# Causal attention: the masked score rows of two heads issued side by side, and whole and masked rows alternating in the order of the maxima

## The reference

```
q, k, v = einsum('bte,hed->bhtd', x, Wq), the same with Wk, Wv     # B 8, T 1024, H 16, d 16
scores = einsum('bhtd,bhsd->bhts', q, k)
scores = where(tril(ones(T, T)), scores, -inf) / sqrt(E)           # E 256
w = softmax(scores, axis=-1)
out = einsum('bhts,bhsd->bhtd', w, v)
```

## Time and profile before

| | |
|---|---|
| median of 3 runs | 5279.27 us (5270.48 to 5296.33) |
| profiled execution | 5293.36 us |
| its span in the trace | 5291.6 us |
| mean granted TensorE clock | 0.892 |
| causal attention in that span | to 1571 us, the steps from 135.6 us |

### The profile page before, as it was taken

How to read it: one execution, slowest core, us unless ns; L and a number is a source line. 1 busy time by engine, 2 the same in 40 slices (tenths; PEclk the granted TensorE clock), 3 DMA queues, 4 the chain that set the end, 5 groups by cost and what they waited for, 6 DMA issues and landing times. The chain is left out here.

```text
span 5291.6 us, 68269 instructions
## 1 busy us (share of the span) xinstructions
PE 4637.5 (88%) x23444; PEld 2457.6 (46%) x23444; DVE 3439.4 (65%) x6212; ACT 2705.4 (51%) x3205; POOL 1377.1 (26%) x1043
## 2 busy tenths in 40 slices
PE   5999999999976888888888888888878999999999
PEld 3544444444433544455445544555543444444443
DVE  5566566656647888878887888455545565565653
ACT  1444444445453344443444344122227888888888
POOL 1011111111112332233233332000004545455454
PEclk7787778778787998999899899999989999999999
DMA  6233222322310000000000000000016766666664
GB/s 166 60 74 64 73 62 62 86 62 72 72 37 15 0 0 0 0 0 0 0 0 0 0 0 0 13 1 0 0 31 156 162 153 144 162 146 154 152 146 110
DMA packets 145900, 322.06 MB, mean 61 GB/s; under 512 B 39504, under 2 KB 64480, under 8 KB 129264
## 3 DMA queue, kind: packets, MB, share of 16 engines
q1 hardware_dynamic: 137664, 310.88, 25.6%
q10 hardware_dynamic: 7920, 7.87, 0.5%
q0 software_dynamic: 64, 0.05, 0.0%
HBM read 237.93 MB, written 80.74 MB: 60 GB/s over the span
## 5 line engine op out<-in xcount | busy, mean ns | idle before, releaser
L1714 ACT ACTIVATE gelu_out<-hidden,b_col 128x1024 f32<-128x1024 f32 x1024 | 1085.4, 1111 | 171.1 <-PE hidden L1628 169.9
L529 ACT ACTIVATE probsT<-scoresT 128x1024 f32<-128x1024 f32 (+3 forms) x768 | 603.8, 810 | 609.7 <-PE scoresT L467 603.9
L577 DVE TENSOR_REDUCE maxima<-front 128x1 f32<-128x512 f32 (+3 forms) x1280 | 735.7, 630 | 274.4 <-PE front L439 177.7
L1694 POOL TENSOR_TENSOR combined<-combined,gated 128x512 f32<-128x512 f32 x480 | 615.6, 1283 | 679.0 <-DVE gated L1812 679.0
L918 POOL TENSOR_TENSOR pair_sums<-sims 128x1024 f32<-128x1024 f32 x256 | 487.9, 1913 | 1140.0 <-DVE pair_exp L1032 777.3
L1812 DVE SCALAR_TENSOR_TENSOR gated<-expert_out,b_col,gates_spread 128x512 f32<-128x512 f32 x480 | 359.1, 748 | 452.1 <-PE expert_out L1638 246.7
L1628 PE MATMUL hidden<-slice_stack,w_stack 128*128 128x512 f32 x2048 | 626.9, 428 | 14.1 <-ACT gelu_out L1714 14.1
L433 PE MATMUL front<-k_stack,q_stack 48*128 48x512 f32 (+3 forms) x1536 | 541.3, 493 | 62.2 <-DVE maxima L577 35.6
L1638 PE MATMUL expert_out<-gelu_out,w_sb 128*32 128x512 f32 x4096 | 547.2, 606 | 31.1 <-DVE gated L1812 26.0
L379 POOL TENSOR_SCALAR_AFFINE_SELECT probsT<-probsT 128x512 f32<-128x512 f32 x256 | 164.7, 644 | 1383.0 <-ACT probsT L529 1383.0
L1628 PEld LDWEIGHTS hidden<-slice_stack,w_stack 128*128 128x128 f32 x2048 | 353.2, 189 | 368.5 <-ACT gelu_out L1714 278.8
(11 more groups left out here) (188 smaller groups left out, 6389.8 us busy)
## 6 DMA issues: line engine op xcount, KB each, us to landing
gates_spread<-gate_scratch SPq DMA_DIRECT2D x512, 256.0 KB, 4.9
stack_scratch<-split_parts SPq DMA_DIRECT2D x192, 256.0 KB, 3.1
slice_stack<-slice_scratch SPq DMA_DIRECT2D x128, 256.0 KB, 7.9
q_stack<-stack_scratch SPq DMA_DIRECT2D x64, 384.0 KB, 6.4
k_stack<-stack_scratch SPq DMA_DIRECT2D x64, 384.0 KB, 9.5
slice_scratch<-slice_parts SPq DMA_DIRECT2D x32, 512.0 KB, 6.3
x_tiles<-in_L_attn_x SPq DMA_DIRECT2D x8, 1024.0 KB, 11.8
out_x<-x_tiles ACTq DMA_DIRECT2D x15, 512.0 KB, 4.7
```

Of the source, the lines that this page charges most:

```text
L529: nc.scalar.activation(PT[:, i % NPT, 2 * pr:2 * pr + 2, at:BANK], ST[pr][:, :, at:BANK], ACT.Exp, scale=SCALE).then_inc(probs_ready, 1)
L577: nc.vector.tensor_reduce(dst, F[k % 3][:, 0:parts * w].rearrange("p (a k) -> p a k", a=parts), AX.X, ALU.max)\
L1694: nc.gpsimd.tensor_tensor(CM[:, par, hc, :], CM[:, par, hc, :], Y[:, u % 2, :], ALU.add)\
L1714: nc.scalar.activation(GH[:, k % 4, :, :], HP[k % HPB][:, :, :], ACT.Gelu, bias=b1c[:, u % E:u % E + 1])\
```

## The change

The list that `maxima` returns is ordered anew: units i and i + 1 of one pair of heads follow one another, then the same two of the other pair of heads. So a whole row (i even) alternates with a diagonal one (i odd) up to i = 7. In `score_rows` the whole rows stay as they were. A diagonal unit is now issued for both heads at its e = 0 turn: PE waits for the banks k and k + 1, and then block by block come the product of head 0 and of head 1, the first mask product of each, the second mask product of each. At the e = 1 turn nothing is issued. The number of instructions and their sizes stay.

```
@@ -157,7 +157,8 @@
 
     def maxima(n, g):
 
-        return [("m", n, g, pr, i, e) for i in range(len(MAXB)) for pr in range(2) for e in range(2)] if n < NS else []
+        return [("m", n, g, pr, i + j, e) for i in range(0, len(MAXB), 2) for pr in range(2) for j in range(2)
+                for e in range(2)] if n < NS else []
 
     def cost(u):
 
@@ -421,24 +422,38 @@
             def score_rows(k, n, g, pr, i, e):
 
                 hf, q = n % 2, 2 * g + pr
-                rows = slice(64 * e, 64 * e + KR)
                 if (pr, i, e) == (0, 0, 0):
                     pe.wait_ge(stacks_in[hf][g], 16 * 4 * (n // 2 + 1))
-                bank_free(k)
                 w = width(*MAXB[i][0])
-                half = slice(64 * e, 64 * (e + 1))
-                for a, (qt, kc) in enumerate(MAXB[i]):
-                    diag = kc == qt // 4
-                    at = (a + 1) * w
-                    mm = nc.tensor.matmul(F[k % 3][:, a * w:at], QS[rows, hf, q, qt * P:(qt + 1) * P],
-                                          KS[rows, hf, q, kc * BANK:kc * BANK + w], start=True, stop=not diag,
-                                          tile_position=(64 * e, 0))
-                    if diag:
-                        nc.tensor.matmul(F[k % 3][:, at - P:at], IH[half, 0, :], MH[half, :], start=False, stop=False,
-                                         tile_position=(64 * e, 0))
-                        mm = nc.tensor.matmul(F[k % 3][:, at - 64:at], IH[half, 1, :], MH[half, 0:64], start=False,
-                                              stop=True, tile_position=(64 * e, 0))
-                mm.then_inc(front_done, 1)
+                diag = MAXB[i][0][1] == MAXB[i][0][0] // 4
+
+                def row_block(e, a, qt, kc):
+                    rows = slice(64 * e, 64 * e + KR)
+                    return nc.tensor.matmul(F[(k + e) % 3][:, a * w:(a + 1) * w], QS[rows, hf, q, qt * P:(qt + 1) * P],
+                                            KS[rows, hf, q, kc * BANK:kc * BANK + w], start=True, stop=not diag,
+                                            tile_position=(64 * e, 0))
+
+                def mask_half(e, a, h):
+                    half = slice(64 * e, 64 * (e + 1))
+                    return nc.tensor.matmul(F[(k + e) % 3][:, (a + 1) * w - P + 64 * h:(a + 1) * w], IH[half, h, :],
+                                            MH[half, 0:P - 64 * h], start=False, stop=(h == 1), tile_position=(64 * e, 0))
+
+                if not diag:
+                    bank_free(k)
+                    k -= e
+                    row_block(e, 0, *MAXB[i][0]).then_inc(front_done, 1)
+                elif e == 0:
+                    bank_free(k)
+                    bank_free(k + 1)
+                    for a, (qt, kc) in enumerate(MAXB[i]):
+                        for e in range(2):
+                            row_block(e, a, qt, kc)
+                        for e in range(2):
+                            mask_half(e, a, 0)
+                        for e in range(2):
+                            mm = mask_half(e, a, 1)
+                            if a == len(MAXB[i]) - 1:
+                                mm.then_inc(front_done, 1)
 
             def turn_maxima(k, n, g):
                 pe.wait_ge(rowmax_ready, 2 * n + g + 1)
```

## The result

The changed kernel takes 5307.1 us (median of 11 runs, 5301.88 to 5313.8) against 5279.27 us before: a ratio of 1.0056, with a 95% interval of 1.0041 to 1.0072. It is slower, by 28 us where 7 were forecast. The time lies in the range of 5230 to 5325, but the likeliest case, no change beyond 0.5%, did not come out; the one that did was given 0.29.

The account below looks back on a forecast made before the run. PE was taken to bound the 16 attention steps, DVE the opening. Terms -12 + 10 + 3 made +1; with the first booked at -6 this became +7, so 5286 us on the median, range 5230 to 5325.

Parts of the forecast that it names:

- the likeliest case: Whole kernel: no change beyond 0.5% (26 us), own range 5265 to 5305 us; chance 0.45.
- the one that did: Whole kernel slower by over 0.5%: chance 0.29, of which 0.02 from the upper tail of the no-change case.
- No gain from interleaving the one-block units: 256 one-block diagonal pairs in attention: heads already run together where both banks are free, so nothing booked.
- the rule of strict order: Diagonal pairs: strict FIFO matmuls would mean a serial chain goes from each pair, -49 us, 5230 us; rival's chance 0.06.
- Two-block units in two slots: 128 two-block diagonal pairs: two slots instead of three; first -12 us (bounds 0 and -51), booked at -6.
- The opening, +10 us: DVE-bound opening at clock 0.50: holes before diagonal pairs count in full, +10 us, bounds +4 and +12.
- The steps, +3 us: The 16 attention steps: dense halves 0.5 us later, step starts 0.2 sooner; +3 us, bounds -15 and +25.
- the waits stay near 190 us: Sign of being right: PE's waits for reductions in attention near 190 us still; below 140 would mean alternation does the work.
- The walk: Changed order followed at two places: step 6's start 0.2 us sooner, a dense second half at 0.50 0.5 later.
- the walk of step 6: Step 6's start: v 0.33 us sooner, next masked pair at 702.14, leaving 0.2 us of gain.
- the slower rival: Attention: holes lengthen low-clock stretches by 15 us in each of 8 batches, 32 us on top of +7, 5318 us; chance 0.27.
- faster by alternation: Attention: narrow reductions or heavy PE units between whole rows spare a quarter of 155.5 us bank waits; 5250 us, chance 0.22.

Follow-up runs that it names:

- the opening undone: Changed kernel, but the diagonal units of step 0 (the opening) issued head by head, in the new order: 5292.65 us, ratio 1.0029 to the kernel before.
- the diagonal unit ahead: New order of the maxima, head by head, with the diagonal unit ahead of the whole one in each couple: 5205.46 us, ratio 0.9874 to the kernel before.
- two-block units side by side: New order, only two-block units side by side, head 0's first product ahead of the wait, one-block units head by head: 5347.16 us, 1.0131 to before.
- one pair of heads after the other: Kernel before, head by head, with all ten units of one pair of heads, then all ten of the other: 5279.88 us, ratio 1.0009.

## Why the prediction was right, and where it was off

**No gain from interleaving the one-block units**: right in the new order with the wait in both kernels, where interleaving all diagonal units gives 2 us; no run has the one-block units alone side by side. With head 0's first product ahead of the wait, interleaving them as well went with 66 us, through a shorter low clock (482 us against 795) that no term of the sum had. The row at 737.15 us had said that the heads overlap already. That is also where the rule of strict order would have led to 5230; it did not come.

**Two-block units in two slots**: the mechanism is in the trace (88.93, 89.37). Its price, booked at -6 us, cannot be read by itself. Interleaving of all diagonal units, behind the wait, measured -23 to -26 in the old order and -2 in the new; the two-block units alone, with head 0's first product ahead of the wait, came out at +119, nearly all of it PE busy time at the low clock.

**The opening, +10 us**: the mechanism is right, its size a little low. Its end moved by 9.4 us (135.6 to 145.0), but that near hit is luck: 3.6 us of the loss were hidden by an earlier start. The opening took 12.9 us more, just past the upper bound of 12. The holes were forecast at 0.6 us for 2 x 128 and 0.8 for 2 x 256, and the two shown are 0.62 and 0.83; their sum at 12, and is 13.6. With the opening undone, the median fell by 14.5.

**The steps, +3 us**: this term was mis-sized, in both of its halves. The profiled steps grew by 3.6 us, which looks like a hit and is luck: it is a sum of -67 from the new order and +71 from the wait with its interleaving. The prediction held that the piece behind a pair starts at about the same time, since PE must reach head 1's bank anyway, and gave as a sign of being right that the waits stay near 190 us. They rose to 407, and PE's idle time in the steps from 59 to 122 us. The walk gave an order no more than tenths of a us in each half step, because it kept the clock as it was; with the new order PE's busy time fell by 71 us at a clock of 0.84 in place of 0.79, and its idle time hardly changed. And the walk of step 6 had left 0.2 us of gain at the next masked pair (702.14 in place of 702.35); in the profile after that pair came 0.03 us later within its step.

**The clock and the slower rival**: that rival has the size (5318 forecast, 5307 measured) but not the way. It wanted longer low stretches than before. In the profile after, low clock is 594.7 us against 604.6, so against before nothing was added; the wait gave back what the order had won. The price of 0.27 us for each us of low clock lies inside what four kernels without the full common wait give against before: 0.38 by the new order, 0.36 with the diagonal unit ahead, 0.33 with two-block units side by side, 0.19 with one pair of heads after the other.

**The rival "faster by alternation"**, 0.22, named a mechanism (spared bank waits) that did not act: they stayed at 190 us. Its side remark, that a shorter low stretch would give the same size, was what the new order alone did. The 0.05 us of handover from a reduction to PE, for which the prediction shows no row, is in the trace: 52 to 53 ns at most of the waits in the kernel before.

What stays open: why one order keeps PE at 1.00 for longer. The common wait raised the low clock in the new order (428 to 590 us) and in the old one by itself (605 to 651), but with interleaving in the old order it did not (565). No run set the clock by itself, so its price is a relation over 13 profiles, not a measured cause. And single executions of one kernel differ by 1% and more (5245.83 to 5299.59 for the kernel before, 5203.06 to 5265.56 for the new order alone); a profile shows one of them. The steps of the new order alone are 67 us shorter in the profiles, where the medians differ by 51 in all. The kernel with head 0's first product ahead of the wait was profiled with a span of 5247.8 us, at a median of 5281.66; its row in the table describes the shortest of its twelve executions.

## What to carry to other kernels

Where two halves of the array are fed from one queue, look first whether their products already start together; if so, writing them side by side in the program has little left to give (here 2 us in one order and some 25 in the other), and a joint wait for both buffers costs what the first half used to do in the meantime. Take the two parts of such a change apart before keeping it: here one was worth -0.87%, the other +0.88%, and the better half was thrown away with the sum. Where PE is the bound and its clock is not full, compare orders by the granted clock of the stretch as well as by waits: the order with the fewest waits was not faster than before, and the fastest one had the highest clock.

## What the hardware showed beyond the expected

- A product of one array half starts ahead of two mask products of the other half that stand before it in the program (737.15 us). The Trainium skill, "TensorE: Matmul & The Clock Gate", Part 3, says that matmuls start in strict order; the starts in this trace do not. In 68 of the 128 pairs of 384-column blocks head 1's product starts ahead of head 0's first mask.
- Reductions of 512 columns that stand in a queue start 0.60 us apart (698.74, 699.35 and 699.95 us in the kernel before) while each is recorded as 0.68 us long.
- Orders of the same products, with no other edit, moved the granted clock of some 1400 us of work from 0.79 to 0.84 and 0.89; with waits and interleaving varied as well it went down to 0.73, and the kernels took from 5205 to 5365 us.
